# A four-layer graph network on one core: the edge net in row groups, the first typed pass by expanded node words, two more picked columns in three passes, and a reordered node stage

## The chip, the core and the metric

One Trainium2 chip, one of its cores. The metric is device microseconds of one execution. Time of the kernel before: 37372.63 us, the median of 3 runs (37361.5 to 37375.28).

## The reference, cut to what matters

12,500 nodes with 16 features, 412,500 edges sorted by destination, four layers, each followed by a residual and a layer norm:

```python
x = _layernorm(x + L0(x))   # out[dst] += x[src] * edge_weight * weight; clip
x = _layernorm(x + L1(x))   # twice: W = relu(edge_attr @ w1 + b1) @ w2 + b2  (16x16 per edge)
                            #        m[e] = x[src[e]] @ W[e]; mean over dst; GRU cell
x = _layernorm(x + L2(x))   # GAT with 3 heads, selu, GAT with 1 head, selu, @ Wf + bf
x = _layernorm(x + L3(x))   # RGCN, 8 edge types: mean over (dst, type) of x[src] @ W[type],
                            # 16 -> 32, relu, 32 -> 16, plus x @ root + bias
```

## The kernel before, in words

The kernel makes seven passes over all edges (k = 0 to 6): k = 0 is layer 0, k = 1 and 2 are the two rounds of layer 1 (the edge net runs in both), k = 3 and 4 the two GAT layers, k = 5 and 6 the two typed layers of layer 3. Edges lie in 128 partitions by T = 3,224 columns, cut into NCH = 62 chunks of TC = 52 columns. Per column the features of 128 source nodes are wanted. They come in one of two ways:

- **gathered**: GpSimd issues one indirect DMA per column (`gathers`, line 529) from a table in HBM into `gb`, which is double-buffered by chunk. A chunk's buffer is freed by `d_gbfree`, which VectorE gives after its last read of it.
- **picked**: the last `OFF[k]` columns of each chunk are made by TensorE. For a pair of columns, SyncE loads 448 KB of one-hots (kept in `oh_d` by pass 0, `KEPT` pairs per chunk), TensorE multiplies them with the packed node table, 7 matmuls per column of 476 columns each in bf16 (`pick_words`, line 732), and VectorE masks each column's result (`keep_words`, line 1106), sums it per pair (`place_words`, line 1112, or in the typed passes `node_words`, lines 1136 to 1142) and decodes it into `gb` (`decode`, lines 1123 and 1127).

`OFF = (20, 12, 12, 16, 14, 16, 14)`, so GpSimd gathers 52 - OFF[k] columns of each chunk.

VectorE then forms the messages of the chunk and sums them by destination with one scan per feature (`sums`, line 1207); steps of the picks (`picks`) are put between the scans and, in passes 1 and 2, between the groups of the net.

**Edge net, passes 1 and 2** (`message_net`, `hidden_units`, `net_pass`). For each eight columns (h): one f32 matmul of 26 rows by 512 columns (`hidden`, line 780), a ReLU on ScalarE into `hid` (line 624). For each four columns (g, 13 per chunk): two f32 matmuls of 128 rows by 512 columns (`weights`, line 789) against `w2as`, whose two halves of 64 rows each fill only their own 256 columns; then VectorE multiplies 1,024 elements out of PSUM (line 1248) and reduces them (line 1251, the last of a chunk on line 1253). `weights(g)` waits until the product of g - 2 has been read. An f32 matmul is two records on TensorE and two weight loads in the trace.

**Typed passes, 5 and 6** (`typed_picks`, `typed_rows`, `typed_step`, `typed_pass`). A picked pair is decoded to node words (16 features), transposed by TensorE (lines 771, 772), copied by ScalarE (line 655), multiplied by all eight types' matrices (lines 762, 763: two f32 matmuls of 16 rows by 256 columns), and VectorE masks the 512 results by type (line 1173) and reduces them into `gb` (line 1176). `typed_pass` multiplies the chunk by the edge's weight on line 1336.

**Node stage after pass 4** (`nodes2b`, `one_head`, `linear_norm`, `tables3`; 7 blocks of 14 node columns). For a block: softmax and selu with two Exps on ScalarE (`one_head`, lines 1515 to 1544), the linear layer on TensorE (`node_product` with `wfs`, transposes line 843, products line 854), its sum and the layer norm (`linear_norm`, line 1626 on), the packing for pass 5, and the table of eight typed products, written to `tab3a` in HBM (`tables3`, line 1602, from products with `l3w1s` on line 854). Passes 5's gathers wait for all of `tab3a`. ScalarE's order by block is: the two Exps, four copies of the linear layer's transposes, a square root, four copies of the table's transposes. VectorE's is `linear_norm(b)`, `one_head(b + 1)`, `pack(b)`, `tables3(b)`.

## Time and profile before

| what | value |
|---|---|
| median of 3 runs | 37372.63 us |
| span of the profiled execution, first to last instruction | 22386.5 us |
| TensorE matmul busy | 18498.7 us (83%) |
| VectorE busy | 18278.4 us (82%) |
| GpSimd busy | 16569.5 us (74%) |
| ScalarE busy | 2764.6 us (12%) |
| HBM traffic over the span | 94 GB/s |

The profiled execution is known by its span; no own time is given beside it. 37372.6 - 22386.5 = 14986.1 us of the runs' time have no instruction in the trace. Busy shares of GpSimd count an indirect DMA of about 0.95 us and leave out the 0.30 us between two of them.

### The profile page before, as it was taken

The page shows a single profiled execution, that of the slowest core. Times are in us where ns is not written, and L with a number is a line of the kernel's source. Part 1 is how long each engine was busy: PE and PEld are TensorE (multiplying, and loading weights), DVE is VectorE, ACT ScalarE, POOL GpSimd, SP SyncE. Part 2 cuts the span into 40 slices and gives each one's busy share as a digit, 9 for nine tenths or more (in the row PEclk, how much of TensorE's full clock was granted, in tenths as well). Part 3 has the DMA queues.
Part 4 walks back from the last instruction along what each step waited for, and adds up shares of the span by engine and source line. Part 5 has one row for each costly group of instructions (what it writes and reads, how often), then busy time and mean ns, then how long its engine had stood idle before and what let it go on. Part 6 is the DMA issues. An engine that isn't in the chain of part 4 may idle for free.

```text
span 22386.5 us, 255590 instructions
## 1 busy us (share of the span) xinstructions
PE 18498.7 (83%) x80302; PEld 8816.9 (39%) x80302; DVE 18278.4 (82%) x37702; ACT 2764.6 (12%) x5989; POOL 16569.5 (74%) x17218
## 2 busy tenths in 40 slices
PE   5577769999979999967777689999788888999996
PEld 2233323333333333344444334444333333544443
DVE  7688879999969999959999877777588888787775
ACT  4466600000010000010000000000100000000000
POOL 6777777777767777767777777777477777677776
PEclk9899989999989999979999799999699999899998
DMA  5344422222222222224444333333233333233332
GB/s 152 101 126 132 131 65 76 76 76 76 72 56 76 76 75 76 74 60 129 128 130 130 85 92 103 103 101 103 74 111 112 112 113 112 75 85 82 83 83 57
DMA packets 1231067, 2116.12 MB, mean 95 GB/s; under 512 B 387306, under 2 KB 743845, under 8 KB 1221293
## 3 DMA queue, kind: packets, MB, share of 16 engines
q1 hardware_dynamic: 677104, 1902.02, 25.8%
q0 software_dynamic: 550848, 196.35, 8.8%
q8 instruction: 670, 10.98, 0.2%
q14 instruction: 656, 5.37, 0.1%
q10 hardware_dynamic: 1789, 1.41, 0.0%
HBM read 1506.14 MB, written 592.22 MB: 94 GB/s over the span
## 4 chain that ended last, share of the span: by engine, by line
POOL 52%; PE 24%; issue 17%; DVE 5%; DVEq 1%; DMA 1%; ACT 0%; ACTq 0%; POOLq 0%; SPq 0%
POOL gb L529 49%; PE psB L789 11%; PE psB L732 8%; PE psA L780 3%; DVE Sb L1207 2%; POOL ext L544 2%; PE psB L854 1%; POOL ext L519 1%; DVE prod L1248 1%; DVE prod L1253 1%; DVEq L1252 1%; PE psA L843 1%; DVE xT L1106 1%; POOL xe2b L550 0%; DVE sub L1059 0%
## 5 line engine op out<-in xcount | busy, mean ns | idle before, releaser
L732 PE MATMUL psB<-xp,arena 128*128 128x476 bf16 x23730 | 5430.4, 376 | 1624.1 <-DVE xT L1106 754.9
L732 PEld LDWEIGHTS psB<-xp,arena 128*128 128x128 bf16 x23730 | 2304.3, 100 | 4914.2 <-issue 2378.9
L732 PE MATMUL psB<-ext,arena 128*128 128x308 bf16 (+1 forms) x17388 | 3198.9, 343 | 733.2 <-DVE xT L1102 670.5
L789 PE MATMUL psB<-w2as,hid 128*128 128x512 f32 x6448 | 3107.8, 608 | 46.4 <-DVE prod L1248 46.4
L529 POOL DMA_INDIRECT gb<-tab1b,srci x2480 | 2406.5, 970 | 780.4 <-issue 752.6
L529 POOL DMA_INDIRECT gb<-tab1a,srci x2480 | 2406.9, 971 | 773.6 <-issue 752.9
L529 POOL DMA_INDIRECT gb<-tab3b,typi x2356 | 2256.5, 958 | 744.1 <-issue 717.5
L529 POOL DMA_INDIRECT gb<-tab3a,typi x2232 | 2179.4, 976 | 848.2 <-issue 679.7
L529 POOL DMA_INDIRECT gb<-tab2b,srci x2356 | 2232.4, 948 | 717.9 <-issue 717.9
L529 POOL DMA_INDIRECT gb<-tab2a,srci x2232 | 2116.2, 948 | 681.2 <-issue 681.2
L732 PEld LDWEIGHTS psB<-ext,arena 128*128 128x128 bf16 x17388 | 1720.2, 100 | 2169.5 <-issue 874.7
L529 POOL DMA_INDIRECT gb<-in_x,srci x1984 | 1911.9, 964 | 668.4 <-issue 604.0
L1248 DVE TENSOR_TENSOR prod<-psB,gb 128x1024 f32<-128x1024 f32 x1612 | 1974.2, 1225 | 527.7 <-PE psB L789 382.3
L1112 DVE TENSOR_REDUCE sub<-xT 128x34 f32<-128x476 f32 (+2 forms) x2294 | 1801.7, 785 | 215.1 <-issue 7.6
L1102 DVE TENSOR_TENSOR xT<-psB,XT 128x616 bf16<-128x616 f32 (+1 forms) x1860 | 1800.5, 975 | 201.2 <-PE psB L732 191.4
L732 PE MATMUL psB<-ext,hid 128*128 128x308 bf16 (+1 forms) x8652 | 1605.8, 342 | 332.5 <-DVE xT L1102 332.5
L1106 DVE TENSOR_TENSOR xT<-psB,sub 128x476 bf16<-128x476 f32 x2728 | 1757.0, 644 | 125.2 <-PE psB L732 109.2
L1251 DVE TENSOR_REDUCE prod<-prod 128x64 f32<-128x1024 f32 x1488 | 1798.4, 1209 | 0.0
L789 PEld LDWEIGHTS psB<-w2as,hid 128*128 128x128 f32 x6448 | 1163.8, 190 | 1580.1 <-issue 1500.8
L732 PE MATMUL psB<-arena,ext 128*128 128x476 bf16 x8120 | 1699.3, 364 | 45.0 <-DVE xT L1102 39.9
L1207 DVE TENSOR_TENSOR_SCAN Sb<-psA,Sb,prod 128x52 f32<-128x52 f32 x6588 | 1674.7, 313 | 17.3 <-issue 0.5
L624 ACT ACTIVATE hid<-psA,b1s 128x512 f32<-128x512 f32 x806 | 553.9, 687 | 5849.5 <-PE psA L780 5849.5
(341 smaller groups left out, 20013.9 us busy)
## 6 DMA issues: line engine op xcount, KB each, us to landing
arena<-oh_d SPq DMA_DIRECT2D x1696, 448.0 KB
hid<-oh_d SPq DMA_DIRECT2D x618, 448.0 KB
oh_d<-arena SPq DMA_DIRECT2D x496, 448.0 KB
ext<-oh_d SPq DMA_DIRECT2D x290, 448.0 KB
S2a<-Sb SPq DMA_DIRECT2D x62, 1404.0 KB
S2b<-Sb SPq DMA_DIRECT2D x62, 884.0 KB
S3a<-Sb SPq DMA_DIRECT2D x62, 832.0 KB
ext<-in_attrT SPq DMA_DIRECT2D x402, 104.0 KB
```

The source lines that it names most:

```text
L529: pool.indirect_dma_start(gb[:, o:o + width], None, table, at(idx[:, t:t + 1])).then_inc(l_gat[k][c % 2], 16)
L544: pool.indirect_dma_start(ext[:, j * f:(j + 1) * f], None, Sd[k], at(endi[:, j:j + 1])).then_inc(l_ends[b], 16)
L624: a.activation(hid[:, (h % 2) * 512:(h % 2 + 1) * 512], psA[h % 2][:, :], ACT.Relu, bias=b1s[:, 0:1]).then_inc(a_hid, 1)
L732: m = pe.matmul(psB[b][:, o:o + W], pk.onehot(n)[:, g, u * P:(u + 1) * P], pk.part(g, q).bitcast(BF16), start=g == 0, stop=g == NB - 1)
L780: pe.matmul(psA[h % 2][:, :], w1s[:, :], atts[q % 3][:, o:o + 512], start=True, stop=True).then_inc(t_hidden, 1)
L789: m = pe.matmul(psB[g % 2][:, i * 512:(i + 1) * 512], hid[:, o:o + P], w2as[:, :], start=True, stop=True)
L1102: v.tensor_tensor(to.rearrange("p (b f x) -> p b f x", b=2, x=2 * JB), psB[b][:, :].rearrange("p (b w) -> p b w", b=2)[:, :, 0:W].rearrang ...
L1106: v.tensor_tensor(v3(to, 2 * JB), v3(psB[b][:, u * 512:u * 512 + W], 2 * JB), spots, ALU.mult).then_inc(d_keep, 1)
L1112: v.tensor_reduce(found(pk)[:, 2 * i * U:2 * (i + 1) * U], v3(words_of(pk.k, n)[:, 0:2 * U * JB], JB), AX.X, ALU.add)
L1207: m = v.tensor_tensor_scan(now[:, :, q], decay(q), data(q), old[:, TC - 1, q:q + 1] if c else 0.0, ALU.mult, ALU.add)
L1248: m = v.tensor_tensor(pr[i % 2], psB[g % 2][:, :].rearrange("p (t o i) -> p t o i", t=4, o=16), bc(gv[:, 4 * i:4 * i + 4, :], 2, 16), ALU. ...
L1251: v.tensor_reduce(msg[:, 4 * i - 4:4 * i, :], pr[(i - 1) % 2], AX.X, ALU.add)
```

## The change

It does five things:

1. `hidden(q)` now makes two blocks of eight columns at once: the edge attributes lie in partitions 0 to 25 and 32 to 57, and two matmuls read 26 rows each, into two PSUM tiles. They signal once.
2. `weights(g)` is four f32 matmuls of 64 rows by 256 columns in place of two of 128 rows by 512: for each of two columns of `hid`, partitions 0 to 63 into one PSUM bank and 64 to 127 into the other.
3. In pass 5 a picked pair's node words are spread over 8 x 16 columns by type (`first_step`), transposed as 128 by 128, multiplied by one matrix of 128 rows by 32 columns, and ScalarE copies the 64 results into `gb` (`typed_out`). VectorE's mask and reduction of 512 elements go.
4. `OFF` becomes (20, 14, 14, 16, 14, 18, 14): two columns of each chunk of passes 1, 2 and 5 are picked and no longer gathered. `KEPT` becomes 9 with it.
5. In the node stage after pass 4, VectorE, ScalarE and TensorE make the linear layer of block b + 1 ahead of the tables of block b, and the Exps of b + 2 stand ahead of the table copies of b.

```diff
@@ -32,7 +32,7 @@
...
-OFF = (20, 12, 12, 16, 14, 16, 14)
+OFF = (20, 14, 14, 16, 14, 18, 14)
...
@@ -400,9 +400,8 @@
 
             def load_att(rep, q):
                 if q >= 3:
-                    sp.wait_ge(t_hidden, NH * rep + 2 * (q - 3) + 2)
-                n = min(1024, NH * 512 - q * 1024)
-                sp.dma_start(atts[q % 3][:, 0:n], attrT[:, q * 1024:q * 1024 + n]).then_inc(l_att[q % 3], 16)
+                    sp.wait_ge(t_hidden, NQ * rep + q - 2)
+                sp.dma_start(atts[q % 3], attrT[:, q * 512:(q + 1) * 512]).then_inc(l_att[q % 3], 16)
 
...
@@ -618,7 +617,7 @@
 
             def hidden_units(rep):
                 for h in range(NH):
-                    a.wait_ge(t_hidden, NH * rep + h + 1)
+                    a.wait_ge(t_hidden, NQ * rep + h // 2 + 1)
                     if h >= 2:
                         a.wait_ge(t_weight, NG * rep + 2 * (h - 1))
                     a.activation(hid[:, (h % 2) * 512:(h % 2 + 1) * 512], psA[h % 2][:, :], ACT.Relu, bias=b1s[:, 0:1]).then_inc(a_hid, 1)
@@ -646,13 +645,42 @@
 
+            def row_copy(pk, m):
+                a.wait_ge(t_turn, pk.typed0 + m + 1)
+                if m >= 2:
+                    a.wait_ge(t_typed, pk.typed0 + m - 1)
+                o, K = (m % 2) * 512, P if pk.k == 5 else pk.F
+                a.activation(pk.xT[0:K, o:o + 2 * P], psA[0][0:K, 0:2 * P], ACT.Copy).then_inc(a_row, 1)
+
+            def typed_out(pk, m):
+                c, i = divmod(m, pk.pairs)
+                a.wait_ge(t_typed, m + 1)
+                if c >= 2:
+                    a.wait_ge(d_gbfree, NCH * 5 + c - 1)
+                a.activation(got(c, 32)[:, TC - pk.off + 2 * i:TC - pk.off + 2 * i + 2, :], v3(psA[1][:, 0:64], 32), ACT.Copy).then_inc(a_got, 1)
+
             def typed_rows(pk):
                 for m in range(pk.last):
-                    a.wait_ge(t_turn, pk.typed0 + m + 1)
-                    if m >= 2:
-                        a.wait_ge(t_typed, pk.typed0 + m - 1)
-                    o = (m % 2) * 512
-                    a.activation(pk.xT[0:pk.F, o:o + 2 * P], psA[0][0:pk.F, 0:2 * P], ACT.Copy).then_inc(a_row, 1)
+                    row_copy(pk, m)
+
+            def first_rows(pk):
+                for n in range(pk.last + 1):
+                    if n:
+                        typed_out(pk, n - 1)
+                    if n < pk.last:
+                        row_copy(pk, n)
+
...
@@ -664,8 +692,22 @@
                     H = 3 if k == 3 else 1
-                if k in (5, 6):
+                if k == 5:
+                    first_rows(PICK[k])
+                if k == 6:
                     typed_rows(PICK[k])
+                if k == 4:
+                    head_exps(0)
+                    linear_rows(0)
+                    head_exps(1)
+                    for b in range(NB):
+                        if b + 1 < NB:
+                            linear_rows(b + 1)
+                        if b + 2 < NB:
+                            head_exps(b + 2)
+                        for g, (j0, cnt) in enumerate(GROUPS):
+                            turned = copy_turned(xT16, 16, g, cnt)
+                    made += 8 * NB
@@ -747,37 +779,49 @@
...
+            def typed_product(pk, m):
+                width = pk.mats.shape[1] // 8
+                pe.wait_ge(a_row, pk.typed0 + m + 1)
+                o = (m % 2) * 512
+                if pk.k == 5:
+                    if m:
+                        pe.wait_ge(a_got, m)
+                    outs, K = [psA[1][:, u * 32:(u + 1) * 32] for u in range(2)], P
+                else:
+                    if m:
+                        pe.wait_ge(d_typed, m)
+                    outs, K = [psA[1][:, u * 8 * width:(u + 1) * 8 * width] for u in range(2)], pk.F
+                for u in range(2):
+                    t = pe.matmul(outs[u], pk.xT[0:K, o + u * P:o + (u + 1) * P], pk.mats, start=True, stop=True)
+                t.then_inc(t_typed, 1)
+
...
+            def turn_pair(pk, m):
+                pe.wait_ge(d_row, pk.typed0 + m + 1)
+                if m:
+                    pe.wait_ge(a_row, pk.typed0 + m)
+                o, K = (1760, P) if pk.k == 5 else (200, pk.F)
+                o += (m + 1) % 2 * 2 * K
+                pe.transpose(psA[0][0:K, 0:P], pk.extra[:, o:o + K], ident)
+                pe.transpose(psA[0][0:K, P:2 * P], pk.extra[:, o + K:o + 2 * K], ident).then_inc(t_turn, 1)
+
...
             def message_net(rep, pk):
-                def hidden(h):
-                    q, o = h // 2, (h % 2) * 512
+                def hidden(q):
                     pe.wait_ge(l_att[q % 3], 16 * (rep * ((NQ + 2 - q % 3) // 3) + q // 3 + 1))
-                    if h >= 2:
-                        pe.wait_ge(a_hid, NH * rep + h - 1)
-                    pe.matmul(psA[h % 2][:, :], w1s[:, :], atts[q % 3][:, o:o + 512], start=True, stop=True).then_inc(t_hidden, 1)
+                    if q:
+                        pe.wait_ge(a_hid, NH * rep + 2 * q)
+                    for u in range(min(2, NH - 2 * q)):
+                        m = pe.matmul(psA[u][:, :], w1s[32 * u:32 * u + 26, :], atts[q % 3][32 * u:32 * u + 26, :], start=True, stop=True)
+                    m.then_inc(t_hidden, 1)
 
                 def weights(g):
                     h = g // 2
@@ -786,12 +830,15 @@
                         pe.wait_ge(d_product, NG * rep + g - 1)
                     for i in range(2):
                         o = (h % 2) * 512 + (g % 2) * 256 + i * P
-                        m = pe.matmul(psB[g % 2][:, i * 512:(i + 1) * 512], hid[:, o:o + P], w2as[:, :], start=True, stop=True)
+                        for u in range(2):
+                            to = u * 512 + i * 256
+                            m = pe.matmul(psB[g % 2][:, to:to + 256], hid[64 * u:64 * u + 64, o:o + P],
+                                          w2as[64 * u:64 * u + 64, 256 * u:256 * u + 256], start=True, stop=True)
                     m.then_inc(t_weight, 1)
 
                 def step(g):
-                    if g % 2 == 0 and g // 2 + 1 < NH:
-                        hidden(g // 2 + 1)
+                    if g % 4 == 2 and g // 2 + 1 < NH:
+                        hidden(g // 4 + 1)
                     weights(g)
 
                 pe.wait_ge(d_nodes, rep + 1)
@@ -906,8 +953,15 @@
                     if k == 4:
-                        turned, made, inputs = node_product(lambda j: h2[:, j, :], 32, 1, xT32, wfs[:, :], 16, b, turned, made, inputs)
-                        turned, made, inputs = node_product(lambda j: xv[:, j, :], 16, 0, xT16, l3w1s[:, :], 256, b, turned, made, inputs)
+                        if b == 0:
+                            turned, made, linear = node_product(lambda j: h2[:, j, :], 32, 1, xT32, wfs[:, :], 16, 0, turned, made, inputs)
+                        if b + 1 < NB:
+                            turned, made, linear = node_product(lambda j: h2[:, j, :], 32, 1, xT32, wfs[:, :], 16, b + 1, turned, made,
+                                                                inputs + 2 + 2 * b)
+                        turned, made, linear = node_product(lambda j: xv[:, j, :], 16, 0, xT16, l3w1s[:, :], 256, b, turned, made,
+                                                            inputs + 1 + 2 * b)
+                        if b + 1 == NB:
+                            inputs += 2 * NB
                     if k == 5:
                         turned, made, inputs = node_product(lambda j: h3[:, j, :], 32, 1, xT32, l3w2s[:, :], 144, b, turned, made, inputs)
 
+
+            def first_step(pk, n, width):
+                if not 1 <= n <= pk.last:
+                    return
+                c, i = divmod(n - 1, pk.pairs)
+                o, e = 200 + (n % 2) * 2 * pk.F, 1760 + (n % 2) * 2 * P
+                node, types = pk.extra[:, o:o + 2 * pk.F], pk.extra[:, 100:100 + pk.off]
+                if i == 0:
+                    tail = slice((c + 1) * TC - pk.off, (c + 1) * TC)
+                    v.drain()
+                    v.scalar_tensor_tensor(types, srci[:, tail], -8.0, typi[:, tail], ALU.mult, ALU.add)
+                    word_masks(pk, c)
+                keep_words(pk, n - 1, 0)
+                keep_words(pk, n - 1, 1)
+                node_words(pk, n, node)
+                v.drain()
+                for u in range(2):
+                    m = v.scalar_tensor_tensor(v3(pk.extra[:, e + u * P:e + (u + 1) * P], 16), bc(io8, 2, 16), types[:, 2 * i + u:2 * i + u + 1],
+                                               bc(node[:, u * 16:(u + 1) * 16], 1, 8), ALU.is_equal, ALU.mult)
+                m.then_inc(d_row, 1)
 
             def picks(k, done, to, width):
-                step = typed_step if k in (5, 6) else half_step
+                step = first_step if k == 5 else typed_step if k == 6 else half_step
                 for n in range(done, to):
                     step(PICK[k], n, width)
                 return max(done, to)
@@ -1332,11 +1405,15 @@
                 done = picks(k, 0, pk.until(-1, 1), width)
                 for c in range(NCH):
                     arrived(k, c)
+                    if k == 5:
+                        v.wait_ge(a_got, (c + 1) * pk.pairs)
                     v.drain()
                     v.tensor_tensor(pr, got(c, width), bc(wE[:, span(c)], 2, width), ALU.mult).then_inc(d_gbfree, 1)
                     v.drain()
                     done = sums(k, c, width, done, range(width), lambda q: pr[:, :, q], lambda q: same[:, span(c)])
                     done = picks(k, done, pk.until(c, 1), width)
+                if k == 5:
+                    v.memset(pk.xT[:, :], 1.0)
 
 
             def fix_sums(k):
@@ -1631,10 +1708,13 @@
             def nodes2b(made, used, acts):
                 v.wait_ge(l_feats, 16)
                 acts = one_head(0, acts)
+                made, acts = linear_norm(0, made, acts)
+                acts = one_head(1, acts)
                 for b in range(NB):
-                    made, acts = linear_norm(b, made, acts)
                     if b + 1 < NB:
-                        acts = one_head(b + 1, acts)
+                        made, acts = linear_norm(b + 1, made, acts)
+                    if b + 2 < NB:
+                        acts = one_head(b + 2, acts)
                     pack(b, xv[:, block(b), :], 16, PICK[5])
                     made, used = tables3(32, b, made, used)
                 return made, used, acts
```

## Rows read from the trace of the kernel before

**Rows 1.** The page: the span, and the chain that ended last by engine.

```profile
span 22386.5 us, 255590 instructions
...
POOL 52%; PE 24%; issue 17%; DVE 5%; DVEq 1%; DMA 1%; ACT 0%; ACTq 0%; POOLq 0%; SPq 0%
```

**Rows 2.** Source view of line 529: min/median/max ns, first to last; idle; waiters.

```profile
L529 POOL DMA_INDIRECT gb<-tab1a,srci x2480: 940/945/3240, 2983.9 to 6149.9; - x191
...
L529 POOL DMA_INDIRECT gb<-tab3a,typi x2232: 938/945/2649, 16207.6 to 19065.8; - x186
...
  issue: 4905.8, 16097
...
  DVE prod L1226: 212.5, 55
```

**Rows 3.** The waits, 3500 to 5500 us (pass 1): total us, times, longest.

```profile
DVE prod L1248 <- PE psB L789: 124.6, 181, 2.0
...
POOL gb L529 <- DVE prod L1253: 5.4, 6, 1.6
```

**Rows 4.** PE's timeline, 4560 us on (pass 1): start, us, what, [idle before].

```profile
4579.88 1.12 PE L780 MATMUL psA<-ext,w1s 26*128 26x512 f32 x2
4580.93 1.98 PE L789 MATMUL psB<-w2as,hid 128*128 128x512 f32 x4
4582.75 1.57 PE L732 MATMUL psB<-xp,arena 128*128 128x476 bf16 x7
4584.15 1.88 PE L789 MATMUL psB<-w2as,hid 128*128 128x512 f32 x4
4585.87 1.57 PE L732 MATMUL psB<-xp,arena 128*128 128x476 bf16 x7
```

**Rows 5.** The timeline of DVE, same stretch.

```profile
4579.44 0.65 DVE L1106 TENSOR_TENSOR xT<-psB,sub 128x476 bf16<-128x476 f32 x1
...
4582.44 0.64 DVE L1106 TENSOR_TENSOR xT<-psB,sub 128x476 bf16<-128x476 f32 x1
...
4583.90 1.23 DVE L1248 TENSOR_TENSOR prod<-psB,gb 128x1024 f32<-128x1024 f32 x1
```

**Rows 6.** The timeline of PE from 17500 us (pass 5).

```profile
17516.62 0.69 PE L762 MATMUL psA<-l3w1f,xT 16*128 16x256 f32 x2
17517.16 0.59 PE L763 MATMUL psA<-l3w1f,xT 16*128 16x256 f32 x2
```

**Rows 7.** The timeline of DVE, same stretch.

```profile
17506.32 0.29 DVE L1170 TENSOR_TENSOR arena<-arena,cst 128x128 f32<-128x128 f32 x1
...
17517.85 0.69 DVE L1173 TENSOR_TENSOR arena<-psA,arena 128x512 f32<-128x512 f32 x1
...
17519.24 1.20 DVE L1106 TENSOR_TENSOR xT<-psB,arena 128x476 bf16<-128x476 f32 x2
...
17521.53 0.19 DVE L1142 SCALAR_TENSOR_TENSOR arena<-arena 128x32 int32<-128x32 int32 x1
```

**Rows 8.** The waits, 16800 to 18800 us (pass 5).

```profile
DVE prod L1336 <- DMA gb<-tab3a,typi: 42.6, 26, 2.8
```

**Rows 9.** The timeline of DVE in the node stage after pass 4.

```profile
16044.10 0.64 DVE L1525 TENSOR_TENSOR ext<-ext,Sb 128x462 f32<-128x462 f32 x1 [11.21 <-ACT Sb L597]
...
16083.40 0.64 DVE L1525 TENSOR_TENSOR ext<-ext,Sb 128x462 f32<-128x462 f32 x1 [11.21 <-ACT Sb L597]
```

**Rows 10.** The timeline of PE, same stage.

```profile
16057.31 1.89 PE L843 MATMUL psA<-cst,arena 128*32 128x128 f32 x8
...
16189.77 3.78 PE L854 MATMUL psB<-l3w1s,xT 16*128 16x256 f32 x8
...
16198.66 5.48 PE L854 MATMUL psB<-l3w1s,xT 16*128 16x256 f32 x12
```

**Rows 11.** The timeline of ACT, same stage.

```profile
16081.85 1.28 ACT L597 ACT_TABLE_LOAD   x1
...
16087.83 0.58 ACT L597 ACTIVATE ext<-ext 128x448 f32<-128x448 f32 x1 [4.47 <-DVE ext L1539]
```

More of the change, by code:

```diff
@@ L260, in gnn_program @@
             sem(f"t_{n}") for n in ("pick", "turn", "typed", "hidden", "weight", "fix", "turned", "made", "mid", "head"))
-        a_hid, a_row, a_exp, a_fixexp, a_turned, a_gate, a_done, a_code = (
-            sem(f"a_{n}") for n in ("hid", "row", "exp", "fixexp", "turned", "gate", "done", "code"))
+        a_hid, a_row, a_exp, a_fixexp, a_turned, a_gate, a_done, a_code, a_got = (
+            sem(f"a_{n}") for n in ("hid", "row", "exp", "fixexp", "turned", "gate", "done", "code", "got"))
         ident = cst[:, CI:CI + P]
@@ L299, in gnn_program @@
         stage = [prod[:, i * 1024:(i + 1) * 1024] for i in range(2)]
-        atts = [ext[0:26, i * 1024:(i + 1) * 1024] for i in range(3)]
+        atts = [ext[0:64, i * 512:(i + 1) * 512] for i in range(3)]
         fwidth = (24, 16, 16, 54, 34, 32, 16)
```

55 lines of the change are left out of this document (21 added, 34 removed).

## The prediction

> **What bounds the kernel now.** First the page: of the span of 22386.5 us the chain that ended last runs 52% on GpSimd and 24% on TensorE [rows 1]. So it must be read pass by pass. The source view of the gathers gives the pace: one lasts 0.945 us at the median and 4905.8 / 16097 = 0.305 us pass before the next, so 1.25 us a column. Pass 1 takes (6149.9 - 2983.9) / 62 = 51.07 us a chunk, which is 40 x 1.25 and 1.07 us over (a gather or two per chunk are long, the maxima of the same rows). Pass 5 takes (19065.8 - 16207.6) / 62 = 46.1 us, 36 x 1.25 and 1.1 over [rows 2]. In both, GpSimd is never short of work. But in pass 1 the other side is just as long: GpSimd waited for VectorE 5.4 us in 2,000, VectorE for TensorE's edge net 124.6 us in the same 39 chunks, 3.2 us a chunk, and never for a gather [rows 3]. Pass 2 is the same code. In pass 5 VectorE does wait for gathers, 42.6 us in 43 chunks, so about 1 us a chunk of slack [rows 8]. In pass 0 VectorE waits for gathers too, before 55 chunks [rows 2].
>
> **The gathers taken away.** Two a chunk in three passes: 62 x 2 x 3 = 372, at 1.25 us 465 us of GpSimd's time, 155 us a pass. That is the most the change can give there; what is late next decides how much it gives.
>
> **Pass 5.** VectorE per pair today, without scans: from 17517.85 to 17521.72, 3.87 us [rows 7]. Of it the mask and the reduction of 512 elements take 1.39 (to 17519.24); they go. Two instructions of 128 elements come; one lasts 0.29, two with their drain about 0.55. So 3.0 us a pair, nine pairs 27.2 in place of eight at 31.0: VectorE's chunk is some 3.5 us shorter, while the gathers' is 2.5 us shorter. TensorE: two f32 matmuls of 256 columns, 0.54 us each by their pitch [rows 6], go for two of 32 columns, and the transposes load 128 columns of weights in place of 16. No row has these. Bounds: between nothing and the 1.08 us that goes, for each pair; I take half, since the loads do not shrink with the columns. A pair's picks are two times 7 matmuls, 2.8 us by the pitch of 1.40 [rows 4], so a pair takes 3.8 us and nine 34.5, against a chunk of 43.6. ScalarE, at a few per cent, takes over a copy of 64 elements. What is queued behind its wait on `d_gbfree` is the next row copy, but the buffer that it asks for was freed a chunk before. So gathers stay the bound: 34 x 1.25 + 1.1 = 43.6 us, **-155 us** for the pass (bounds -100 and -155). The fill after the last chunk, 1,024 elements, costs no more than the 1.23 us of a 1,024-element product [rows 5], once.
>
> **Passes 1 and 2, VectorE.** A further pair costs it a mask (0.65 and a drain), and a mask with the sum of the pair, 1.46 (4582.44 to 4583.90) [rows 5], together 2.2; decode and masks grow by a sixth, 0.1. Today's chunk is 51.07, of which 3.2 are waits for TensorE. If these all go: 51.07 - 3.2 + 2.3 = 50.2 us. GpSimd's would be 38 x 1.25 + 1.07 = 48.6. So VectorE becomes the bound at 50.2, and the two gathers give 0.9 us a chunk, not 2.5: 124 x 0.87 = **-108 us** (down to 0 if TensorE stays late as now, -310 if VectorE were no bound, which its rows exclude).
>
> **Passes 1 and 2, TensorE.** Today: the two matmuls of a group have a pitch of 1.72 us alone (4584.15 to 4585.87) and 1.82 after the 26-row one, a column's picks 1.40, eight columns' hidden layer 1.05 (4579.88 to 4580.93) [rows 4]. A chunk: 13 x 1.77 + 12 x 1.40 + 6.5 x 1.05 = 46.6 of 51.07, the rest being waits while VectorE scans. After, no row shows two matmuls in the array at a time. Upper bound, they do not share it: a group is four times the 0.54 of an f32 matmul of 256 columns [rows 6], 2.16, and the chunk is 13 x 2.16 + 14 x 1.40 + 6.8 = 54.5 busy, 59 with the same waits. Lower bound, each pair runs fully side by side: 13 x 1.08 + 19.6 + 3.4 = 37.0. I take a value in between: an f32 matmul is two passes over the same rows, so only the second of one and the first of the other can overlap while starts stay in order; four matmuls then take 5 of 8 steps, 1.3 us a group, and the hidden layer 3 of 4. To this I add 0.2 us at each group for the change of shape: around the 26-row matmul of today the neighbours are 0.10 and 0.19 us late [rows 4]. That is 13 x 1.5 + 19.6 + 5.1 = 44 us, 48 with the waits, under VectorE's 50.2.
> The Trainium skill bears on this in two places. "TensorE: Matmul & The Clock Gate", Part 3, says that matmuls in distinct row groups overlap, with 3.07x measured for four of 32 rows, though starts and ends keep program order; "TensorEngine Tiling (Array Packing)", Key Properties, says that changing the mode drains the array, which speaks against groups of 64 rows between picks of 128. With the first alone the sum stays as it is, since VectorE bounds. The second has no price on its page.
>
> **Node stage after pass 4.** A block takes 39.3 us (16044.10 to 16083.40), in which VectorE waits 11.21 for an Exp [rows 9] queued on ScalarE behind the table's copies. That wait goes, but the cycle has TensorE in it twice. From the end of the tables' products (16057.31 [rows 10]) linear layer, norm and the start of the next head run to 16072.19 (16083.40 - 11.21): 14.9. Then ScalarE's table load, 1.28 [rows 11], and the first Exp, an estimate of 0.4; the head up to its second Exp and that Exp, to 16088.41, 5.0 [rows 9, 11]; then the copies, 0.7, that now stand behind it; then the products of one table, 16189.77 to 16204.14, 14.4 [rows 10]. Sum 36.7 a block, 2.6 less. Over the five blocks that have such a head 13 us, and the ends even out: **-12 us** (bounds 0 and 7 x 11.2 = -78).
>
> **Pass 0** writes one more pair of 448 KB per chunk, 62 in all. VectorE and SyncE have the gathers as cover there [rows 2]; without cover it is a wait of a microsecond or two each. Taken at 0, bound +60.
>
> **The sum.** -155 - 108 - 12 + 1 = -274 us on a span of 22386.5, so 22113. The runs' median is 37372.6, 14986 us above the span; nothing in the trace says what these are. I leave them as they are: **37099 us**, 0.73% faster. Two times of this kernel less than 0.2% (75 us) apart I count as equal.
>
> **The rivals.**
> *The bound stays TensorE in passes 1 and 2* (change of shape dearer than 0.2 us, or less overlap): from 46 us busy a chunk on, the waits come back. At 51 to 52 us a chunk passes 1 and 2 give 0 to +110, in total about -110, **37260**. For it: today's sum is within 1 us of deciding. Against: it needs 0.2 us a group more than I allow. Chance 0.15. The drain of which the Trainium skill speaks in "TensorEngine Tiling (Array Packing)", Key Properties, would act in this way; no row shows it at 64 rows.
> *The row groups do not share the array:* TensorE at 59 us a chunk, 8 more than now, 124 times: +980; with pass 5's -155 and the node stage's -12 **38190**, slower. It decides from about 2.0 us a group on. For it: no row of before has two at a time. Chance 0.12.
> *Pass 5 gives nothing,* because its longer round (word, spread, transpose, copy, product, copy out) or a wait for `a_got` makes TensorE late: -119 in all, **37254**. Against: the steps run two ahead of the chunk. Chance 0.08.
> *The time outside the span moves as well.* If the runs stretch the gathers (14986 us over 16,097 of them [rows 2] is 0.93 us each), 372 fewer give 2.18 us each, 810 in all, **36560**. If it goes with the bytes of inputs or scratch in HBM, which grow (attributes by a fifth, one-hots by an eighth), it could as well be slower. Nothing in the trace speaks for either. Chance 0.1, two thirds of it faster.
> *The forecast:* chance 0.55, by itself 37030 to 37170.
> The range, 36950 to 37290, takes in the first and third rivals, and below the forecast the node stage's bound (66 us more) and a part of what passes 1 and 2 give if VectorE's rows shrink somewhat (half of the 202 us between its 108 and 310). Faster by over 0.2%: 0.55 + 0.10 + 0.07 + 0.07 = 0.79; within 0.2%: 0.05 from the edges of the first and third; slower 0.16.
>
> **What would show it.** Right: in passes 1 and 2 a chunk of 50 us, VectorE without waits for the edge net, GpSimd now waiting for VectorE about 1.6 us a chunk; four records of 256 columns and their partners starting within a few ns of each other; in pass 5 a chunk of 43.6 us with gathers back to back; in the node stage 37 us a block, no wait of 11 us. Wrong: VectorE's waits for the edge net at 3 us a chunk or more, group pitches near 2.1 us, or a difference of spans that isn't the difference of the times.

## The result, and the profile after

The changed kernel takes **36998.57 us** (median of 4 runs, 36984.5 to 37013.0) where the kernel before takes 37370.65 (4 runs): ratio 0.9903 [0.9891, 0.9915], 372 us faster. The forecast was 37099 with a range of 36950 to 37290. The number lies inside; the sum behind it is another matter, as the page of the profiled execution shows.

Page of the kernel after: the span, the chain that ended last by engine, and (source view of line 528) the gathers of pass 1 and of pass 5: min/median/max ns, first to last:

```profile
span 37011.7 us, 276253 instructions
...
another core or an unknown queue 32%; DVE 26%; PE 21%; issue 14%; DVEq 6%; ACT 1%; DMA 0%; POOL 0%; ACTq 0%; SPq 0%; POOLq 0%
...
L528 POOL DMA_INDIRECT gb<-tab1a,srci x2356: 938/944/2582, 4769.4 to 10034.0; - x197
...
L528 POOL DMA_INDIRECT gb<-tab3a,typi x2108: 940/944/1079, 26505.4 to 31004.8; - x192
```

The span is 37011.7 us and this execution's own time 37013.0. **Nothing lies outside the span.** The 14,625 us by which this span is longer than that of [rows 1] is inside the passes: pass 1 takes (10034.0 - 4769.4) / 62 = 84.9 us a chunk, not 51, with gathers of the same 0.944 us. GpSimd, half of the chain in [rows 1], has no share in it now; for 32% of the chain the profile names no releaser on this core. So the trace before the prediction and the runs whose median was to be predicted were two different ways in which the same program runs. The experiments, made in four groups with the kernel before in each, met both: in two groups it took 22380 and 22384 us, with a trace like the one of before (below: **regime A**), in the two others 37305 and 37307 us (**regime B**, as in the result). The same chip number is on record with either regime, so whether it is the chip or its condition is not settled. Both regimes are followed below; every ratio is taken within one of them.

The whole change was also met in regime A (run a3): 22204.06 us against 22380.38, ratio 0.992 [0.9903, 0.9937], 176 us faster. Its page and gathers:

```profile
span 22202.6 us, 276253 instructions
...
POOL 51%; issue 17%; DVE 17%; PE 9%; DVEq 5%; DMA 0%; ACT 0%; ACTq 0%; POOLq 0%; SPq 0%
...
L528 POOL DMA_INDIRECT gb<-tab1a,srci x2356: 940/944/2522, 2983.3 to 6143.9; - x197
...
L528 POOL DMA_INDIRECT gb<-tab3a,typi x2108: 940/944/2657, 16171.5 to 18882.9; - x192
```

These answer [rows 1, 2]: pass 1 is 50.98 us a chunk (51.06 before), pass 5 43.73 (46.1 before). The same lengths, first gather to last divided by 62, worked out for the traces at hand (us a chunk; last column: from the last gather of pass 4 to the first of pass 5, us):

```
regime, kernel (OFF of passes 1,2,5)   pass 0  1      2      3      4      5      6      node stage
A before            (12,12,16)         45.06   51.06  51.08  45.10  47.56  46.10  47.95  323.7
A after, run a3     (14,14,18)         45.03   50.98  50.92  45.15  47.53  43.73  47.93  300.9
B node_only         (12,12,16)         71.66   84.21  83.60  75.48  78.04  79.37  87.25  437.0
B after, run a1     (14,14,18)         71.88   84.73  85.03  75.46  78.00  72.36  87.23  438.0
```

node_only is the kernel before with the new node stage alone, and so all its seven passes are those of before. It stands in here because there is no trace of the kernel before in regime B. One caution for the last digit: passes 1 and 2 of a like kernel (typed_node, below) took 84.25 and 84.25 us in another group of runs, so up to 0.65 us a chunk can differ between groups.

### The profile page after: what moved, and what is told of

Read it like the earlier page. It is cut to its first block, busy times and chain, and to the rows that moved or that the text cites. A ratio compares the mean times of both kernels' runs of the same rounds, so it can differ in the third digit from the quotient of the medians.

```text
span 37011.7 us, 276253 instructions
## 1 busy us (share of the span) xinstructions
PE 19835.6 (54%) x89726; PEld 9384.5 (25%) x89726; DVE 18318.8 (49%) x38447; ACT 2910.9 (8%) x6609; POOL 16095.0 (43%) x16846
## 4 chain that ended last, share of the span: by engine, by line
another core or an unknown queue 32%; DVE 26%; PE 21%; issue 14%; DVEq 6%; ACT 1%; DMA 0%; POOL 0%; ACTq 0%; SPq 0%; POOLq 0%
PE psB L764 17%; DVE Sb L1280 5%; DVE xT L1160 4%; DVE prod L1321 4%; DVE sub L1166 2%; DVEq L1165 2%; DVE xT L1156 2%; PE psB L835 2%; DVEq L1189 1%; DVE arena L1127 1%; PE psB L901 1%; DVE arena L1190 1%; PE psA L795 1%; DVE prod L1324 1%
## 5 line engine op out<-in xcount | busy, mean ns | idle before, releaser
L764 PE MATMUL psB<-xp,arena 128*128 128x476 bf16 x26040 | 6967.2, 421 | 5890.9 <-DVE xT L1160 3205.7
L764 PE MATMUL psB<-ext,arena 128*128 128x308 bf16 (+1 forms) x17388 | 3599.5, 357 | 2903.7 <-issue 2291.2
L764 PEld LDWEIGHTS psB<-xp,arena 128*128 128x128 bf16 x26040 | 2625.3, 108 | 9904.3 <-issue 7375.5
L1160 DVE TENSOR_TENSOR xT<-psB,sub 128x476 bf16<-128x476 f32 x2976 | 1916.5, 645 | 4114.7 <-remote 3498.9
L835 PE MATMUL psB<-w2as,hid 64*128 64x256 f32 x12896 | 2166.5, 454 | 2048.8 <-issue 1201.3
L528 POOL DMA_INDIRECT gb<-tab3a,typi x2108 | 1996.9, 947 | 2733.2 <-DVE prod L1411 1879.7
L764 PE MATMUL psB<-arena,ext 128*128 128x476 bf16 x8120 | 1982.6, 391 | 1430.9 <-issue 867.2
L764 PE MATMUL psB<-ext,hid 128*128 128x308 bf16 (+1 forms) x8652 | 1811.9, 356 | 1424.8 <-issue 1196.3
L835 PEld LDWEIGHTS psB<-w2as,hid 64*128 64x128 f32 x12896 | 1346.1, 215 | 3079.3 <-issue 2460.7
L1160 DVE TENSOR_TENSOR xT<-psB,arena 128x476 bf16<-128x476 f32 x1116 | 681.9, 641 | 2173.0 <-remote 1906.9
```

The lines of the kernel that those rows point to most:

```text
L528: pool.indirect_dma_start(gb[:, o:o + width], None, table, at(idx[:, t:t + 1])).then_inc(l_gat[k][c % 2], 16)
L764: m = pe.matmul(psB[b][:, o:o + W], pk.onehot(n)[:, g, u * P:(u + 1) * P], pk.part(g, q).bitcast(BF16), start=g == 0, stop=g == NB - 1)
L835: m = pe.matmul(psB[g % 2][:, to:to + 256], hid[64 * u:64 * u + 64, o:o + P], w2as[64 * u:64 * u + 64, 256 * u:256 * u + 256], start=True, ...
L1160: v.tensor_tensor(v3(to, 2 * JB), v3(psB[b][:, u * 512:u * 512 + W], 2 * JB), spots, ALU.mult).then_inc(d_keep, 1)
```

## What regime B is, read from its trace

Three engines of the kernel after during one chunk of pass 1. GpSimd (start, us, what, [idle before]):

```profile
7079.34 0.96 POOL L528 DMA_INDIRECT gb<-tab1a,srci  x1 [38.30 <-DVE prod L1326]
...
7126.85 0.95 POOL L528 DMA_INDIRECT gb<-tab1a,srci  x1 [0.30 <-issue]
7164.66 0.95 POOL L528 DMA_INDIRECT gb<-tab1a,srci  x1 [36.86 <-DVE prod L1326]
```

TensorE and then VectorE:

```profile
7097.33 1.36 PE L764 MATMUL psB<-xp,arena 128*128 128x476 bf16 x6 [1.72 <-issue]
7099.36 0.36 PE L764 MATMUL psB<-xp,arena 128*128 128x476 bf16 x1 [0.67 <-issue]
7108.55 2.04 PE L835 MATMUL psB<-w2as,hid 64*128 64x256 f32 x6 [8.82 <-issue]
...
7126.11 2.14 PE L764 MATMUL psB<-xp,arena 128*128 128x476 bf16 x5 [12.13 <-issue]
7130.89 1.25 PE L764 MATMUL psB<-xp,arena 128*128 128x476 bf16 x2 [2.65 <-issue]
```

```profile
7107.18 1.23 DVE L1321 TENSOR_TENSOR prod<-psB,gb 128x1024 f32<-128x1024 f32 x1 [10.00 <-remote]
7108.32 1.21 DVE L1324 TENSOR_REDUCE prod<-prod 128x64 f32<-128x1024 f32 x1
7125.31 0.65 DVE L1160 TENSOR_TENSOR xT<-psB,sub 128x476 bf16<-128x476 f32 x1 [15.78 <-remote]
```

And the two stretches of that chunk, with the gathers and without, then the first of them cut in two (us; busy us and instructions of TensorE, its weight loads, VectorE, ScalarE and GpSimd; granted clock, DMA share, GB/s):

```profile
7079.30:7126.90 47.60, 19.34 (x82) 8.99 (x83) 18.65 (x35) 0.69 (x1) 36.29 (x38) 0.66 0.18 39
7126.90:7164.70 37.80, 27.44 (x134) 12.33 (x132) 29.67 (x32) 4.12 (x6) 0.94 (x2) 0.84 0.21 67
...
7079.30:7096.90 17.60, 13.61 (x64) 6.29 (x64) 14.72 (x31) 0.69 (x1) 13.60 (x14) 0.81 0.34 89
7096.90:7126.90 30.00, 5.73 (x18) 2.70 (x19) 3.93 (x5) 0.00 (x0) 22.69 (x25) 0.58 0.10 10
```

The 38 gathers run at their full pace, 1.25 us each, in one burst. During it VectorE is busy 18.65 of 47.6 us, but not evenly: 14.72 of the first 17.6 us, as in regime A, and 3.93 of the 30.0 after them. In these 30 us TensorE and VectorE stand still for 9 to 16 us at a time with no instruction named that they wait for (issue, remote). Shorter halts fall within a group of seven matmuls, where no wait stands in the code: 6 and 1 with 0.67 us between, 5 and 2 with 2.65. VectorE's last halt (7.13 us) ends at 7133.83, 7 us after the last gather was issued; from then on it is busy nearly all the time, and GpSimd sits idle 36.86 us until the buffer is free. The chunk is no exception: averaged over 60 chunks of the pass VectorE is busy 87% of the first 15 us of a burst, 10% from 20 to 50 us after its start and 96% from 55 us on; in pass 5 the fall comes after 10 us. VectorE's work in the whole chunk, 48.3 us, is what it does in a chunk of 51 us in regime A (47.4 on the average of pass 1), where it goes on beside the gathers. So a chunk costs about its gathers' time *plus* most of the others' work, and not the longer of the two: only the first 10 to 15 us of a burst are shared. The DMA engines aren't full (share 0.18).

The node stage after pass 4 shows the same without picks. Two stretches of the kernel after in regime B, the first with a burst of GpSimd's indirect DMAs (79 of its instructions), the second with none; then the first one's counterpart in regime A (run a3), with 79 too; and VectorE's copies of two neighbouring blocks in the second stretch:

```profile
26150.00:26250.00 100.00, 9.94 (x42) 7.84 (x42) 8.13 (x21) 4.22 (x7) 74.94 (x79) 0.50 0.12 14
...
26350.00:26450.00 100.00, 72.34 (x241) 50.63 (x241) 50.19 (x136) 22.53 (x38) 0.00 (x0) 0.50 0.12 49
```

```profile
15900.00:16000.00 100.00, 46.99 (x176) 34.42 (x176) 39.32 (x110) 19.30 (x32) 75.86 (x79) 0.50 0.17 32
```

```profile
26342.96 1.29 DVE L1679 COPY prod<-psB 128x512 f32<-128x512 f32 x2
...
26377.98 1.29 DVE L1679 COPY prod<-psB 128x512 f32<-128x512 f32 x2
```

Beside the same 79 indirect DMAs VectorE is busy 39.32 us of 100 in regime A and 8.13 in regime B. Without GpSimd a block takes 26377.98 - 26342.96 = 35.0 us, exactly what it takes in regime A (below), at the same granted clock of 0.50. So regime B is not explained by a slower clock or engine: it is slower while GpSimd issues indirect DMAs and for some us after, and there alone in the stretches read here. (TensorE's clock does fall in its halts; see the last section.)

As for a cause, I compared the ends of TensorE's and VectorE's halts of over 3 us between 6000 and 9000 us with the starts of the packets that load instructions: the median distance is about 11 us for TensorE and 13 for VectorE, that of random moments about 9. So the start of such a packet is not what ends a halt. What does, stays open. Nor is there an execution without a trace to compare: each timed execution of the result has its span on record, so whether the recording takes part in the halts is not tested.

**Two accounts** were carried through the experiments. *Theory 1*, the prediction's: GpSimd, VectorE and TensorE run beside one another and the longest sets the chunk. *Theory B*: gathers hold the others up, and the times add. (Two expectations use "Theory 2" for a theory of their own, told there.)

## The experiments

### Regime A: the change with the old numbers of picked columns

```diff
-OFF = (20, 14, 14, 16, 14, 18, 14)
+OFF = (20, 12, 12, 16, 14, 16, 14)
```

> The changed kernel with OFF as before, (20, 12, 12, 16, 14, 16, 14): edge net, first typed pass and node stage stay, the 372 gathers come back. By the prediction (gathers or VectorE bound a chunk, the longer of the two): passes 1 and 2 go back to 51.07 us a chunk and pass 5 to 46.1, so all but the node stage's 12 us is lost, 37360. By the rival that in these runs the time of a chunk's gathers and VectorE's work on it add up: passes 1 and 2 lose 2.5 us of gathers and win 2.3 of VectorE, nothing; pass 5 loses 2.5 and wins 3.0, so 36970, within 0.1% of after.

Measured: 22334.25 us against 22384.11, ratio 0.9978 [0.9969, 0.9988]; 50 us faster. (The kernel before, traced again beside it, run b0: 22378 us, span 22377.0, like [rows 1]. Of the two theories written down for it, one that 14,984 us lie outside the instructions and one that gathers hold the engines up, neither could be tested there, since no time was missing.) Its waits between 3500 and 5500 us (pass 1), and from 16800 to 18800 (pass 5):

```profile
DVE prod L1321 <- DMA gb<-tab1a,srci: 98.0, 39, 5.1
...
DVE prod L1411 <- DMA gb<-tab3a,typi: 481.8, 43, 12.0
```

Both are new: in pass 1 VectorE waits for gathers 98.0 / 39 = 2.5 us a chunk, where it waited for the edge net 3.2 [rows 3]; in pass 5 481.8 / 43 = 11.2, where it was about 1 [rows 8]. The net side by side and the lighter first typed pass leave the gathers as they are, and the gathers are then late: pass 1 is 50.82 us a chunk and pass 5 46.41. The gain of 50 us lies in the node stage (323.7 to 300.8), passes 1 and 2 (29 us) and between the passes, less 19 us by which pass 5 is longer. Theory 1 holds here: little is won in passes 1 and 2, and nothing in pass 5, until gathers are taken away.

### Regime B: the whole change, and parts of it

> The whole change, unchanged, where before takes 22384 us. Theory 1 (the longer of gathers and VectorE sets a chunk, as in the prediction): with off_old's rows VectorE needs 50.82 - 2.5 + 2.3 = 50.6 us a chunk in passes 1 and 2, so only 0.2 us a chunk less than off_old there, and pass 5 goes from 46.4 to 43.9: 22334 - 25 - 155 = 22155, 1.0% under before. Rival (gathers' time and VectorE's add up): 22330, as off_old. If the chip is one on which before takes 37.37 ms: 37000 again.

Measured: 36953.05 us against 37306.96, ratio 0.9907 [0.989, 0.9923], and in another group of runs (a2) 36940.2 against 37305.15. Both were in regime B, so theory 1's 22155 was not at stake; the ratio is the result's.

Two fewer picked columns in pass 5 and in passes 1 and 2 in turn, all else as in the change:

```diff
-OFF = (20, 14, 14, 16, 14, 18, 14)
+OFF = (20, 14, 14, 16, 14, 16, 14)    net14
+OFF = (20, 12, 12, 16, 14, 18, 14)    off5_18
```

> The whole change, but OFF (20, 14, 14, 16, 14, 16, 14): pass 5 picks 16 columns. Theory 1: passes 1 and 2 at 50.6 us a chunk, pass 5 at 46.4, 22310 us against off_old's 22334; GpSimd waits for VectorE some 2 us a chunk. Theory 2 (VectorE's chunk in passes 1 and 2 grows past the old one, since the picks' masks wait for TensorE): 51.5 us a chunk and more, 22400. Where before takes 37.37 ms: equal to a1 within 0.2% if the gain there comes from pass 5's lighter VectorE work, 0.4% above it if it comes from the gathers taken away.

Measured: 36867.12, ratio 0.9884 [0.9867, 0.99]. Without the two columns that the change takes from the gathers of pass 5 the kernel is 86 us *faster*; the pass is 71.2 us a chunk, not 72.4. Neither value written down for this regime foresaw that: equal within 0.2%, or 0.4% slower.

> The whole change, but OFF (20, 12, 12, 16, 14, 18, 14): passes 1 and 2 pick 12 columns as before. Theory 1: pass 5 at 43.9 us a chunk, passes 1 and 2 at 50.82, 22180 us; only 25 us above a1. Theory 2: below a1, near 22170 or less, since VectorE has slack in passes 1 and 2 again. If pass 5's longer round were the bound, its chunk would stay at 46 and the time at 22330.

Measured: 37030.91, ratio 0.9928 [0.9912, 0.9945]; passes 1 and 2 at 85.5 and 85.4 us a chunk, 0.8 and 0.4 above the whole change. Here two more gathers a chunk cost 78 us in all. Its expectation had no value for this regime.

Only the node stage (VectorE's part of the edit is shown; ScalarE's and TensorE's orders change with it):

```diff
                 acts = one_head(0, acts)
+                made, acts = linear_norm(0, made, acts)
+                acts = one_head(1, acts)
                 for b in range(NB):
-                    made, acts = linear_norm(b, made, acts)
                     if b + 1 < NB:
-                        acts = one_head(b + 1, acts)
+                        made, acts = linear_norm(b + 1, made, acts)
+                    if b + 2 < NB:
+                        acts = one_head(b + 2, acts)
```

> The kernel before with the node stage after pass 4 reordered and nothing else. By the prediction a block takes 36.7 us, not 39.3, and the stage is 12 us shorter. By off_old's trace, whose gap between the gathers of passes 4 and 5 is 300.8 us against 323.9, it is 23 us shorter. The rest of the time is as before: 22361 to 22372. Nothing if the Exp's wait only moves to the table products.

Measured: 37276.43 against 37306.96, ratio 0.9996 [0.9986, 1.0005]: not told from no change; the 22361 to 22372 were for regime A. Its gathers of passes 1 and 5, in regime B as the kernel before has them, and those of net14 in pass 5:

```profile
L529 POOL DMA_INDIRECT gb<-tab1a,srci x2480: 938/944/2587, 4731.1 to 9952.2; - x191
...
L529 POOL DMA_INDIRECT gb<-tab3a,typi x2232: 938/944/1173, 26319.3 to 31240.4; - x186
```

```profile
L528 POOL DMA_INDIRECT gb<-tab3a,typi x2232: 940/944/1100, 26451.6 to 30866.4; - x186
```

With the same 2,232 gathers pass 5 goes from 4921.1 to 4414.8 us: **506 us, all of the gain and more, come from the new typed step**, 8.2 us a chunk for eight pairs. It is lighter for two engines: over the pass VectorE's busy time falls from 2327.1 to 1954.7 us, 6.0 a chunk, and TensorE's from 2568.8 to 2123.4, 7.2 a chunk. No run takes one without the other, so which of them counts is not shown. In regime A the same edit alone gave nothing (46.10 to 46.41). One pair more and two gathers fewer (a1 against net14) then cost 1.15 us a chunk. In passes 1 and 2 off5_18 differs from node_only by the net alone, and is 1.3 and 1.8 us a chunk *longer* (85.50 and 85.40 against 84.21 and 83.60), 192 us in all: the net side by side, which takes VectorE's waits away in regime A, is a loss here.

### Regime B: the change without its edge net, and fewer picks still

The net of before (two matmuls of 128 rows a group, its hidden layer and its attributes' layout too, of which the main lines are shown) and the old OFF, with the new typed pass and node stage:

```diff
-                        for u in range(2):
-                            to = u * 512 + i * 256
-                            m = pe.matmul(psB[g % 2][:, to:to + 256], hid[64 * u:64 * u + 64, o:o + P],
-                                          w2as[64 * u:64 * u + 64, 256 * u:256 * u + 256], start=True, stop=True)
+                        m = pe.matmul(psB[g % 2][:, i * 512:(i + 1) * 512], hid[:, o:o + P], w2as[:, :], start=True, stop=True)
...
-OFF = (20, 14, 14, 16, 14, 18, 14)
+OFF = (20, 12, 12, 16, 14, 16, 14)
```

> The kernel before with the first typed pass and the node stage of the change; edge net and OFF as before. Theory B (where before takes 37.3 ms, gathers hold the other engines up, and a chunk is the gathers' time plus most of the others' work): passes 1 and 2 stay at 84.2 and 83.6 us a chunk as in node_only, pass 5 goes from 79.4 to net14's 71.2: 37276 - 506 = 36770, below both a2 and net14. Rival: the edge net's side-by-side form is worth something there too, then it is 36950 or more. Where before takes 22384 us the gathers bound pass 5 and passes 1 and 2 are as before: 22360.

Measured: 36755.04 against 37305.15, ratio 0.9852 [0.9836, 0.9869]; theory B had said 36770. It is 185 us faster than the whole change beside it (a2). Passes 1 and 2 are 84.25 us a chunk, 1.2 below off5_18, which differs in them by the net alone: the loss by the net once more, in another group of runs.

Fewer picks in passes 3 to 6:

```diff
-OFF = (20, 14, 14, 16, 14, 18, 14)
+OFF = (20, 14, 14, 14, 12, 16, 12)
```

> The whole change, but OFF (20, 14, 14, 14, 12, 16, 12): against net14 two picked columns fewer in passes 3, 4 and 6, so 372 more gathers. Theory B (the times add): a gather costs 1.25 us, a picked pair costs VectorE about 3.3 us in passes 3 and 4 and 5 in pass 6, so 0.8, 0.8 and 2.5 us a chunk are won: 36867 - 250 = 36620. Rival (gathers bound the chunk): 465 us more than net14, 37330. Where before takes 22384 us, the rival's mechanism is the one expected: some 450 us above net14's 22310.

Measured: **36496.54**, ratio 0.9786 [0.977, 0.9802], 444 us faster than the whole change beside it and 2.1% faster than before. Pass 6 after, and in this run:

```profile
L528 POOL DMA_INDIRECT gb<-tab3b,typi x2356: 940/944/1060, 31349.2 to 36761.4; - x197
```

```profile
L528 POOL DMA_INDIRECT gb<-tab3b,typi x2480: 940/944/1075, 31062.5 to 36238.8; - x191
```

124 gathers more, 155 us at 1.25, and the pass is 5176.3 us long instead of 5412.2. In theory 1 that cannot be. In theory B a picked pair (each of the passes 3 to 6 has one a chunk fewer) must cost more on the other engines than its 2.5 us of gathers; here it costs 2.5 + 3.8 = 6.3 us. The size was underrated (36620 expected), the direction is as theory B says. Pass 4 goes from 78.0 to 76.55. Pass 3, 75.46 to 75.21, gains almost nothing: its pair costs about what its gathers do.

### Regime A: still fewer picks, the whole change, and half the gathers

The last group of runs was to carry theory B further, but met regime A. First, on typed_node:

```diff
-KM = 20
+KM = 16
...
-OFF = (20, 12, 12, 16, 14, 16, 14)
+OFF = (16, 12, 12, 12, 10, 14, 10)
```

> The edge net of the kernel before, the new first typed pass, the new node stage, and OFF = (16, 12, 12, 12, 10, 14, 10): up to four picked columns a chunk fewer than the kernel before in pass 0, 3, 4 and 6, two fewer in pass 5; the one-hots kept are 7 pairs a chunk. Theory B (where before takes 37300 us, a chunk costs the gathers' time and most of the other engines' time on top): each pair taken out of the picks gives 1 to 2 us a chunk net of its 2.5 us of gathers. From the run off_less (36497): the old net gives 0.5 to 1.0 us a chunk in passes 1 and 2 (-60 to -120), two columns fewer in pass 4 and in pass 6 each -90 to -230, pass 3 nothing to -20, pass 5 nothing to -50, pass 0 -100 to +100: about 36150 us. Theory 1 (the longer of GpSimd and VectorE is the bound, the rest lies beside it): gathers bind passes 0, 3, 4, 5, 6, so 2.5 us a chunk more for each pair taken out, that is (2+2+2+1+2) pairs against before, 62 x 2.5 x 9 = 1395 us slower than before, less nothing.

Measured: 23735.81 against 22380.38, ratio 1.0604 [1.0586, 1.0622]: 1355 us slower, where theory 1 had said 1395. Pass 6 (42 gathers) is 53.05 us a chunk, 42 x 1.25 and 0.55. The step of off_less, fewer picks for more gathers, which made the kernel 1.2% faster in regime B, costs 2.5 us for each pair in regime A. In regime B this kernel was not met; the 36150 us are open.

Then the whole change as it is:

> The whole change once more, in case this chip is of the kind on which the kernel before takes 22384 us. There theory 1 expects passes 1 and 2 at 50.2 us a chunk or less and pass 5 at 43.6 us, 22110 to 22150 us in all, ratio 0.988 to 0.990. Where before takes 37300 us: 36950 us as before.

Measured as told in the result: 22204.06, 54 us above the upper end of theory 1's bracket; pass 5 came as expected (43.73), passes 1 and 2 did not (50.98 and 50.92, not 50.2 or less). Waits from 3500 to 5500 us:

```profile
POOL gb L528 <- DVE prod L1326: 110.0, 39, 4.5
...
DVE prod L1321 <- PE psB L835: 30.5, 22, 2.8
```

GpSimd now waits for VectorE 110.0 / 39 = 2.8 us a chunk (5.4 in all in [rows 3]): VectorE is the bound, as forecast.

Last, every second gather of passes 5 and 6 left out (the count for which VectorE waits is halved with it, not shown), so the kernel leaves out work and is no candidate:

```diff
-                    for i in range(TC - OFF[k]):
+                    for i in range(0, TC - OFF[k], 2 if k > 4 else 1):
```

> The whole change, with every second gather of passes 5 and 6 left out (17 in place of 34 and 19 in place of 38 a chunk; the features of those columns are then not the reference's). Theory B, where before takes 37300 us: times add, so pass 5 falls by 17 x 1.25 = 21 us a chunk, from 72.4 to about 51, and pass 6 by 19 x 1.25 = 24, from 87.2 to about 63; in all 45 x 62 = 2800 us less, 34150 us. Rival (everything on such a chip is simply slower, the gathers lie beside): no change of the chunk, 36950 us. Theory 1 on a chip where before takes 22384 us: pass 5 falls from 43.6 to VectorE's own time, 38 to 43 us, pass 6 likewise, about -5 to -600 us in all.

Measured: 21780.58, ratio 0.9731 [0.9714, 0.9747]. Waits from 16800 to 18800 us (pass 5):

```profile
POOL gb L528 <- DVE prod L1411: 789.3, 45, 20.9
```

With 17 gathers a chunk GpSimd waits 17.5 us a chunk for VectorE, and pass 5 is 37.7 us a chunk, pass 6 45.6, in place of 43.7 and 47.9. Theory 1 holds: what is left is the pace of VectorE with its own waits. In regime A 21 and 24 us of gathers a chunk lie beside other work, and taking them away gives 6 and 2.3 us.

## Point by point: why the prediction was right in its number and wrong in its sum

**The span and the 14986 us: the step that failed, and luck.** "I leave them as they are" took the two to be one execution and something around it. They are two regimes. Nothing of the runs' time lies outside the span (37011.7 of 37013.0), and no term of the sum was read from a trace of the runs to be predicted. That the number came within 100 us is luck: in regime B the terms were otherwise. By the passes of a1 against node_only, pass 5 gave -435 (forecast -155) and passes 1 and 2 +121 (forecast -108); the rest between passes and in pass 0 is near zero, and the node stage alone is the -30 of node_only, within the measurement (-12). By parts it is further off still. The gathers taken away, to which the sum gave all its -263 in the passes, gave about nothing: +72 us in pass 5 (a1 against net14), -71 in passes 1 and 2 (a1 against off5_18). The lighter typed step, which by the sum gives nothing as long as gathers are the bound, gave -506, and the net side by side, of which the sum only asked that it be quick enough, cost 192. The hint was there: a time 1.67 times the span of its own trace is no overhead around a kernel. The prediction gave it one rival of 0.10, whose stretched gathers (2.18 us each) did not come either: a gather takes 1.25 us in both regimes, and it is the others that are stretched.

**In regime A, where the rows were valid, the terms can be judged.** Sum forecast -274, measured 22204 - 22380 = **-176**. Pass 5 gave 147 of it, the node stage 23, passes 1 and 2 together 15.

- *Pass 5*: right. 43.73 us a chunk against 43.6, 2858.2 to 2711.4 = -147 against -155; gathers back to back; VectorE's own chunk 37.7 (half56), well under. The slack was underrated: with the old OFF VectorE waits for gathers 11.2 us a chunk (off_old), and about 1 us of slack and eight pairs at 0.87 are 8. The waits of before from 16800 to 18800 us hold the rest, which the sum passed over: VectorE waited for TensorE's typed product, 108.7 / 43 = 2.5 us a chunk, and this wait is gone in off_old and a3.

```profile
DVE arena L1173 <- PE psA L763: 108.7, 68, 2.4
```

- *Passes 1 and 2, VectorE*: the bound moved to VectorE as forecast. Its own chunk, 50.95 less the 0.8 us of waits (30.5 / 39), is 50.1 against the 50.2 of the sum. But the waits for the edge net that were to go entirely leave that 0.8, and so the two passes give 5 and 10 us, not 54 each. The mechanism held, the term was mis-sized (15 us for 108): a gain of 0.87 us that is the difference of two sums of 50 stands or falls with each 0.8.
- *Passes 1 and 2, TensorE*: the assumed 1.3 + 0.2 us a group was too dear. TensorE in a3 from 4576 us on:

```profile
4575.34 1.13 PE L823 MATMUL psA<-ext,w1s 26*128 26x512 f32 x4
4576.40 1.13 PE L835 MATMUL psB<-w2as,hid 64*128 64x256 f32 x8
4577.57 1.57 PE L764 MATMUL psB<-xp,arena 128*128 128x476 bf16 x7
4579.06 1.13 PE L835 MATMUL psB<-w2as,hid 64*128 64x256 f32 x8
```

  The hidden layer's four records take 1.06 us to the next start, where its two of before took 1.05 ([rows 4]); a group of eight takes 1.17 with the picks behind it (1.72 for the four of before), the picks 1.49 (1.40). The two matmuls of a pair start 6 or 7 ns apart in this trace. So two matmuls of 64 rows lie side by side, near the lower bound of the prediction (1.08), and the change of shape costs about 0.1 us each way. The step in which only half of each pair overlaps was wrong. A chunk of pass 1 has TensorE busy 41.8 us, against the 44 of the sum. The rival in which the row groups do not share the array is out. Part 3 of "TensorE: Matmul & The Clock Gate" in the Trainium skill says that distinct row groups overlap, and the trace agrees: eight records of 256 columns, 2.16 us one after another by the pitch of [rows 6], pass in 1.17. The Trainium skill's "TensorEngine Tiling (Array Packing)", Key Properties, says that a change of tiling mode drains the array; here that can be at most those 0.1 us.
- *Node stage*: forecast 36.7 us a block and -12, measured 35.0 and **-23**. VectorE's copies of two neighbouring tables in a3, and between them the instruction of [rows 9] that waits for the Exp:

```profile
16048.67 1.29 DVE L1679 COPY prod<-psB 128x512 f32<-128x512 f32 x2 [3.25 <-PE psB L901]
...
16069.68 0.64 DVE L1602 TENSOR_TENSOR ext<-ext,Sb 128x462 f32<-128x462 f32 x1 [0.29 <-ACT Sb L596]
...
16083.68 1.29 DVE L1679 COPY prod<-psB 128x512 f32<-128x512 f32 x2 [3.02 <-PE psB L901]
```

  The 11.21 us of [rows 9] are gone, as said: the same instruction waits 0.29 us for its Exp. What was wrong was to put ScalarE's table load and the first Exp (1.7 us) into the cycle; 36.7 less that is the 35.0 measured. The term was mis-sized, -12 for -23. In regime B the block is 35.0 us too, and the gain of the stage alone, 30 us of 37307, is within the measurement.
- *Pass 0*: 45.06 to 45.03 with one more pair written a chunk. Right.

**The rivals in regime A**: TensorE does not stay the bound; pass 5 does give. In regime B none of these describes what happened, since they presuppose that the engines run beside one another.

**What none of the runs settles**: what holds the engines from some 10 to 15 us into a burst of gathers on, and what sets the regime; whether recording the trace takes part; whether shorter bursts, with pauses between, would avoid it; why the net side by side costs 1.2 to 1.8 us a chunk in regime B (a group is 8 records instead of 4; that the number of instructions counts there is argued, not shown); and typed_node and off_less in regime A, half56 and best in regime B.

## What to carry to other kernels

Lay the profiled execution's own time beside its span before any sum: if the runs' median is far from it, the rows describe another execution, and the split of work between engines must be tried on the one that is timed. A load moved from gathers to TensorE and VectorE is a gain only where the two run beside each other and the gathers are the longer; where gathers hold the others up it has to be weighed pair by pair as a sum, and work taken off VectorE and TensorE counts (8.2 us a chunk here for 6.0 and 7.2 of busy time). A gain that is the difference of two bounds within 1 us of each other in a chunk of 50 is unsafe: 15 of the 108 us came.

## What the runs showed of the hardware

- The same program takes 22.38 or 37.31 ms, steady to 0.3% within a group of runs. In the slower kind GpSimd's indirect DMAs keep their 1.25 us, and the other engines run beside them for the first 10 to 15 us of a burst and then crawl: VectorE is busy 14.72 of the first 17.6 us and 3.93 of the next 30.0. In 100 us of the node stage with 79 such DMAs VectorE is busy 8 us, in the faster kind 39.
- Two f32 matmuls in distinct row groups cost together about what one costs: 1.06 us for four records of 26 rows by 512 columns (1.05 for two before), 1.17 for eight of 64 rows by 256 columns with matmuls of 128 rows behind them.
- The halts cost TensorE its clock as well. Three stretches of the chunk above (columns as there):

```profile
7090.00:7096.00 6.00, 5.60 (x32) 2.51 (x30) 4.56 (x5) 0.00 (x0) 4.48 (x6) 1.00 0.13 22
7108.50:7111.00 2.50, 2.04 (x6) 1.48 (x7) 1.03 (x1) 0.00 (x0) 1.89 (x3) 0.50 0.07 7
...
7139.70:7150.00 10.30, 9.97 (x58) 4.91 (x57) 9.87 (x12) 1.37 (x2) 0.00 (x0) 1.00 0.20 52
```

  It is granted 1.00 (2.4 GHz) while it works 5.60 of 6 us, 0.50 (1.2 GHz) right after the halt of 8.82 us, when six records take 2.04 us, and 1.00 again from 7139.70 on, when eight take 1.13. Over the whole of pass 1 the mean is 0.74, in regime A 0.92.
